# The eight causal lags of a grouped recurrence: sixteen bf16 products over 128 rows, or two sets of four fp32 products over 32 rows each, with a new order of the steps around them

## The reference

```python
ctx = causal_ema(x, tau_ctx)
wg = sigmoid(concat([x, ctx]) @ Wg.T + bg)
gated = x * wg
h1 = gelu(x @ Wn1.T + bn1)                       # 32 hidden values a token
mod = 0.5 + sigmoid(h1 @ Wn2.T + bn2)            # 32 modulations a token
traces = causal_ema(gated * mod[d], tau[d])      # for each of the 32 decays d
temporal = sum_d traces[d] * softmax(blend)[d]
gate = sigmoid(temporal @ Wtemp.T + btemp)
soma = gelu(x @ Wsoma.T + bsoma)
x = x + layernorm((soma * gate) @ Wout.T)
```

## Time and profile before

| | us |
|---|---|
| median of 3 runs (range) | 328.15 (328.13 to 328.81) |
| profiled execution | 326.89 |
| its span | 325.0 |
| front and step 0, TensorE busy | 34.41 of 39.42 |
| steps 1 to 6, TensorE busy | 112.09 of 115.92 |
| end section and attention, TensorE busy | 159.64 of 169.66 |
| steps 1 to 6, VectorE / ScalarE / GpSimd busy | 97.53 / 68.13 / 81.45 |

### The profile page before, as it was taken

How to read it: one execution, slowest core, us unless ns; L and a number is a source line. 1 busy time by engine, 2 the same in 40 slices (tenths; PEclk the granted TensorE clock), 3 DMA queues, 4 the chain that set the end, 5 groups by cost and what they waited for, 6 DMA issues and landing times. The chain is left out here.

```text
span 325.0 us, 9974 instructions
## 1 busy us (share of the span) xinstructions
PE 306.1 (94%) x3314; PEld 207.0 (64%) x3324; DVE 274.6 (85%) x1449; ACT 215.2 (66%) x459; POOL 248.8 (77%) x300
## 2 busy tenths in 40 slices
PE   8898899999999999999887989999999999999995
PEld 2554464656566465555535667887887887887873
DVE  3888899878978886797879669999999999999972
ACT  5862256545655655457674678878778878778863
POOL 3173586778686885665855869999999999999990
PEclk9999999999999999999999999999999999999999
DMA  6700120050311305013530435564544364210011
GB/s 184 222 2 1 32 67 34 17 130 3 105 42 57 90 0 144 4 33 65 75 60 2 87 95 83 82 139 126 126 105 117 93 126 105 78 32 6 3 34 34
DMA packets 29154, 23.07 MB, mean 71 GB/s; under 512 B 2736, under 2 KB 27824, under 8 KB 29104
## 3 DMA queue, kind: packets, MB, share of 16 engines
q1 hardware_dynamic: 29104, 22.44, 29.3%
HBM read 7.75 MB, written 2.10 MB: 30 GB/s over the span
## 5 line engine op out<-in xcount | busy, mean ns | idle before, releaser
L1609 POOL TENSOR_TENSOR arena<-arena,neg_max 128x512 f32<-128x512 f32 x128 | 129.9, 1052 | 10.8 <-DVE neg_max L1451 10.7
L1451 DVE CUSTOM_DVE_ANT_0 arena<-ps,arena 128x128 f32<-128x128 f32 x512 | 113.9, 287 | 9.6 <-issue 5.1
L1093 ACT ACTIVATE arena<-ps 128x512 f32<-128x512 f32 x128 | 69.6, 596 | 10.2 <-PE ps L789 10.2
L789 PE MATMUL ps<-ident_sb,arena 128*128 128x128 f32 x512 | 68.2, 276 | 0.0
L789 PEld LDWEIGHTS ps<-ident_sb,arena 128*128 128x128 f32 x512 | 56.5, 141 | 6.9 <-POOL arena L1609 4.0
L1528 POOL TENSOR_TENSOR arena<-arena 128x448 f32<-128x448 f32 (+6 forms) x56 | 42.8, 764 | 23.2 <-DVE arena L1283 19.6
L1451 DVE DVE_READ_ACCUMULATOR2_ANT neg_max<- 128x1 f32 x512 | 42.6, 83 | 0.0
L805 PE MATMUL ps<-arena 128*32 128x128 f32 x1024 | 41.2, 279 | 0.0
L1515 POOL TENSOR_TENSOR arena<-decay_a,arena 128x192 f32<-128x192 f32 x32 | 19.5, 637 | 22.0 <-ACT arena L930 22.0
L805 PEld LDWEIGHTS ps<-arena 128*32 128x32 f32 x1024 | 24.1, 109 | 6.9 <-issue 0.3
L775 PE MATMUL ps<-arena 48*128 48x128 bf16 x512 | 25.4, 219 | 2.4 <-DVE neg_max L1451 2.3
(11 more groups left out here) (172 smaller groups left out, 575.4 us busy)
## 6 DMA issues: line engine op xcount, KB each, us to landing
arena<-q_parts SPq DMA_DIRECT2D x96, 64.0 KB
arena<-k_parts SPq DMA_DIRECT2D x96, 64.0 KB
arena<-in_x SPq DMA_DIRECT2D x16, 256.0 KB, 3.3
arena<-in_xt SPq DMA_DIRECT2D x8, 256.0 KB, 2.8
out<-arena SPq DMA_DIRECT2D x7, 256.0 KB, 3.0
arena<-in_consts SPq DMA_DIRECT2D x1, 420.0 KB, 3.8
w_sb<-in_w SPq DMA_DIRECT2D x1, 384.0 KB, 6.3
w_sb<-in_w SPq DMA_DIRECT2D x1, 192.0 KB, 4.1
```

Of the source, the lines that this page charges most:

```text
L789: mm = pe.transpose(ps[1][:, q % 2, k * P:k * P + P], neg_t[q % NT_RING][:, k * P:k * P + P], ident)
L1093: act.activation(probT[q % PT_RING], ps[1][:, q % 2, :], ACT.Exp, scale=-1.0)\
L1451: dve.tensor_tensor_reduce(out=neg_t[q % NT_RING][:, cs], in0=ps[0][:, score_bank(c) + slot, cs], in1=nbias[n % 2], scale=1.0, scalar=3.0e ...
L1609: pool.tensor_tensor(t4, t4, neg_max[:, n % 2, 4 * z:4 * z + 4].unsqueeze(2).broadcast_to([P, 4, P]), ALU.subtract).then_inc(s["shifted"], 1)
```

## The change

1. *Lags.* Groups 0 to 7 all use fp32 weights `w_lag` and the fp32 tanh `thd`, on 32 rows a lag. `four_lags` issues four products, lag k of the set on partitions 32k to 32k+31, each into its own bank: lags 0, 1, 6, 7 in banks 0 and 1 of the group's half, lags 2 to 5 in banks 2 and 3 of the other half. All functions that split weights or modulations are gone, and each lag has its own `prod`.
2. *Banks.* The temporal gate uses bank 0 (where the cross products were), the context bank 3, the values bank 3.
3. *Order.* The hidden product (with Wn1) of group g+2 and the query product stand ahead of the output product of group g; the soma product stands behind the local products; on VectorE and ScalarE the steps are re-ordered likewise, and `late_tables` stands ahead of `b_mixed`, the logarithm behind `c_values`.
4. *Step 0* has an order of its own, with a product whose result nobody reads (384 columns) ahead of the output.

```diff
@@ TensorE @@
+            def four_lags(i, m, first):
+                u = m % 2
+                if first == 0:
+                    pe.wait_ge(s["soma_ready"], grp(i, m, 1, 1))
+                    pe.wait_ge(s["modn_ready"], grp(i, m, 1, 1))
+                    if at_start(i, m, 1):
+                        pe.wait_ge(s["vec_step"], vec("lag_c"))
+                        pe.wait_ge(s["h1_ready"], 2)
+                    else:
+                        pe.wait_ge(s["bh_ready"], grp(i, m, NJ + NCAR))
+                else:
+                    pe.wait_ge(s["prod_ready"], grp(i, m, Q, 4))
+                for lag in range(first, first + 4):
+                    rows_of = slice((lag - first) * D, (lag - first) * D + D)
+                    pe.matmul(lag_bank(m, lag), w_lag[rows_of, lag, :], thd[u][rows_of, :], start=True, stop=True)\
+                        .then_inc(s["lag_ps"], 1)
...
-                    pe.wait_ge(s["modT_tanh"], grp(i, m, 1, 1))
...
+                    pe.wait_ge(s["centred"], grp(i, m, GB, -GB))
                 four(ctx_bank(i, m), lambda cs: xn[u][:, cs], lambda cs: lt[:], "ctx_ps")
...
             def b_locals(i, m):
+                if not at_start(i, m, 2):
+                    pe.wait_ge(s["part3_ready"], grp(i, m, 2, -2))
...
             def b_out(i, m):
+                if not last_group(i, m):
+                    pe.wait_ge(s["prod_ready"], grp(i, m, Q, Q + 6))
...
+            def first_step(i, m):
+                b_locals(i, m)
+                f_modulation_n(i, m + 1)
+                f_gate_ctx(i, m + 1)
+                value_bias()
+                b_cross(i, m)
+                four_lags(i, m + 1, 0)
+                b_crossT(i, m)
+                f_gated(i, m + 1)
+                b_gate(i, m)
+                four_lags(i, m + 1, 4)
+                pe.wait_ge(s["gn_ready"], 2)
+                pe.matmul(bank(1, 2)[:, 0:W_FIRST * P], wt["wg_x"], w_sb[:, 0:W_FIRST, :].rearrange("p k c -> p (k c)"),
+                          start=True, stop=True)
+                b_out(i, m)
+                f_hidden(i, m + 2)
+
+            def step(i, m):
...
+                f_modulation(i, m + 1)
+                b_carries(i, m)
+                f_gate_x(i, m + 1)
+                f_context(i, m + 1)
+                b_locals(i, m)
+                f_soma(i, m + 1)
+                f_modulation_n(i, m + 1)
+                f_gate_ctx(i, m + 1)
+                c_x1T(i, m - 1)
+                four_lags(i, m + 1, 0)
+                f_gated(i, m + 1)
+                b_cross(i, m)
+                c_k(i, m - 1)
+                b_crossT(i, m)
+                four_lags(i, m + 1, 4)
+                c_less(i, m - 1, 1, 0)
+                b_gate(i, m)
+                c_less(i, m - 1, 1, 1)
+                c_q(i, m - 1)
+                if not last_group(i, m + 1):
+                    f_hidden(i, m + 2)
+                b_out(i, m)
+                c_less(i, m - 1, 0, 0)
+                c_v(i, m - 1)
+                c_less(i, m - 1, 0, 1)
@@ ScalarE, step @@
-            def f_mod_part1(i, m):
-            def f_mod_part1b(i, m):
...
+                c_part(i, m - 1, 1, 2)
+                c_part(i, m - 1, 0, 0)
+                if not last_group(i, m + 1):
+                    f_hidden(i, m + 2)
+                c_part(i, m - 1, 0, 1)
+                c_values(i, m - 1)
                 if i * 2 + m == COUNTED:
                     act.wait_ge(s["vec_step"], vec("cnt_none"))
                     act.activation(lncnt[:], cnt1[:], ACT.Ln).then_inc(s["lncnt_ready"], 1)
-                if closes:
-                    c_values(i, m - 1)
+                c_part(i, m - 1, 0, 2)
@@ VectorE @@
-            def lag_parts():
-            def f_mod_parts(i, m):
...
+                b_carries(i, m)
+                if at_start(i, m, 2):
+                    key_tables()
                 b_locals(i, m)
                 f_gated(i, m + 1)
+                f_lags(i, m + 1, range(0, 4))
+                b_temporal(i, m)
+                f_lags(i, m + 1, range(4, 6))
                 if first < last:
                     counts(first)
                 if 2 * i + m == COUNTED:
                     late_tables()
+                b_mixed(i, m)
+                f_lags(i, m + 1, range(6, Q))
                 if first < last:
                     counts(first + 1)
                 c_moments(i, m)
+                c_centre(i, m)
@@ GpSimd, step @@
+                f_lags(i, m + 1, range(1, 6))
                 if first < last:
                     counted(first)
+                f_lags(i, m + 1, range(6, Q))
+                c_rstd(i, m)
                 if first < last:
                     counted(first + 1)
```

More of the change, by code:

```diff
@@ L174, in build @@
             gn.append(take(W))
-            prod.append([take(W), take(W)])
+            wide, temporal, two = take(W), take(W), take(W + P // 2)
+            third, fifth, sixth = 5 * W // 8, 3 * W // 8, 2 * W // 8
+            prod.append([None, wide, temporal, two[:, 0:third], two[:, third:], wide[:, 0:fifth],
+                         wide[:, fifth:fifth + sixth], temporal])
             modn.append(take(P))
-            weights_at = at[0] - 4 * W - P
         xn = [take(W) for _ in range(2)]
@@ L188, in build @@
         take(NU * W)
[L189 to L191 removed]
+        crn, temporalT, sg, ln = gn, [p[2] for p in prod], gT, acc
         vx = [take(2 * VS) for _ in range(2)]
@@ L252, in ctx_bank, with lag_bank, gate_bank @@
         def ctx_bank(i, m):
-            return bank(1 if at_start(i, m, 1) else m % 2, 1)
+            return bank(1, 1) if at_start(i, m, 2) else bank(m % 2, 3)
+        def lag_bank(m, lag):
+            return bank(m % 2, lag % 2) if lag in (0, 1, 6, 7) else bank(1 - m % 2, 2 + lag % 2)
+        def gate_bank(i, m):
+            return bank(m % 2, 2 if last_group(i, m) else 0)
         def at_start(i, m, before):
@@ L411, in _ @@
             for _ in range(12):
-                pe.matmul(bank(1, 3), mod_pb[0][:, 0:P], mod_pb[0][:], start=True, stop=True)
+                pe.matmul(bank(1, 3), zeros[:, 0:P], zeros[:, 0:W], start=True, stop=True)
             pe.wait_ge(s["small_loaded"], 32)
@@ L593, in b_gate @@
                 pe.wait_ge(s["temporal_ready"], grp(i, m, 1, 1))
-                pe.matmul(bank(u, 2), wt["wtemp"], temporalT[u], start=True, stop=True).then_inc(s["temp_ps"], 1)
+                pe.matmul(gate_bank(i, m), wt["wtemp"], temporalT[u], start=True, stop=True).then_inc(s["temp_ps"], 1)
             def b_out(i, m):
@@ L730, in repeat @@
                 for _ in range(times):
-                    pe.matmul(bank(0, 2), lag_a[:, 0, :], mod_pa[1][:], start=True, stop=True)
+                    pe.matmul(bank(0, 2), q_parts[:, 0, 0:P], q_parts[:, 0, 0:W], start=True, stop=True)
             def end():
@@ L944, in b_gate @@
                 act.wait_ge(s["temp_ps"], grp(i, m, 1, 1))
-                act.activation(bank(u, 2), bank(u, 2), ACT.Tanh, bias=hb[:, 1:2], scale=0.5).then_inc(s["temp_tanh"], 1)
+                act.activation(gate_bank(i, m), gate_bank(i, m), ACT.Tanh, bias=hb[:, 1:2], scale=0.5).then_inc(s["temp_tanh"], 1)
             def c_x1T(i, m):
@@ L1317, in b_mixed @@
                 dve.wait_ge(s["temp_tanh"], grp(i, m, 1, 1))
-                dve.scalar_tensor_tensor(sg[u], bank(u, 2), 1.0, somaT[u], ALU.add, ALU.mult)\
+                dve.scalar_tensor_tensor(sg[u], gate_bank(i, m), 1.0, somaT[u], ALU.add, ALU.mult)\
                     .then_inc(s["mixed_ready"], 1)
@@ L1378, in step @@
                 first, last = FIRST_QUAD[2 * i + m], FIRST_QUAD[2 * i + m + 1]
-                if closes:
-                    b_carries(i, m)
-                    f_mod_parts(i, m + 1)
+                if not closes:
+                    b_locals(i, m)
+                    f_gated(i, m + 1)
+                    row_factors()
+                    f_lags(i, m + 1, range(0, 2))
+                    b_temporal(i, m)
+                    f_lags(i, m + 1, range(2, 4))
+                    dve.wait_ge(s["const_ps"], 2)
+                    dve.wait_ge(s["rows_loaded"], 16)
+                    pro("kept_bias", dve.tensor_tensor(kept_bias[:], bank(1, 3)[:, 0:P], bo, ALU.add), waited=False)
+                    b_mixed(i, m)
+                    f_lags(i, m + 1, range(4, Q))
+                    c_moments(i, m)
+                    c_centre(i, m)
+                    return
+                b_carries(i, m)
+                if at_start(i, m, 2):
+                    key_tables()
                 b_locals(i, m)
-                if not closes:
-                    row_factors()
                 f_gated(i, m + 1)
-                f_lags(i, m + 1, range(0, 2))
+                f_lags(i, m + 1, range(0, 4))
+                b_temporal(i, m)
+                f_lags(i, m + 1, range(4, 6))
                 if first < last:
```

239 lines of the change are left out of this document (58 added, 181 removed).

## The result

The changed kernel takes 324.13 us (median of 4 executions, 323.15 to 324.38) and the kernel before 328.48 (4 executions, 328.13 to 329.01): 4.35 us less, ratio 0.986, 95% interval 0.983 to 0.989. I had forecast 9.7 us less.

The account below looks back on a forecast made before the run. The prediction took TensorE to bound the groups' stretch. Steps 7.4 us, front 3.4 and the way from last output to end section 0.4, less 1.5 at the end, gave 9.7: 328.15 becomes 318.5 us, range 313.5 to 324.5.

Parts of the forecast that it names:

- sign: Whole kernel: faster by more than 0.2% at 91%, slower by more at 7%, no change at 2%.
- overlap: Lag products on TensorE: a set of four on separate rows was to overlap and take 1.0 us.
- Front and end: Before the first output and in the end section: 3.4 us gained at the front, 1.5 lost at the end.
- Step 6: Last step of the groups: late tables just ahead of the mixing were to lose 0.6 us.
- New order: Reordered steps, followed from the modulation products: a step of 17.9 us, with 17.1 of TensorE work and 0.8 of waiting.
- The order's waits eat TensorE's gain: Local products and output: late waits paid in full, 1.0 us more per step, 324.5 us; chance 17%.
- The late input: Hidden product's input for the group after next: one us late in five steps, 323.5 us; chance 5%.
- TensorE alone decides: Steps and end: only 17.1 us of TensorE work per step stays, the end loses nothing, 312.2 us; chance 11%.

Follow-up runs that it names:

- e5_adj: On e2_swap: turned modulation moved right behind the local products, soma next to the gate product, query product beside the temporal gate's; 318.47 us, ratio 0.971.
- e1_pad: Changed kernel with 22 instead of 11 repeated products in the end section, keeping TensorE busy until the turned x1 of group 6; 321.05 us, ratio 0.980.
- e10_idle: On e2_swap: the 11 repeated products ahead of the turned residual of group 6 removed, so TensorE idles there; 322.33 us.
- e9_fill: On e8_mixfirst: 5, 3 and 4 repeated bf16 products put in three idle stretches of the octets' second and third step; 317.76 us.
- e2_swap: Changed kernel with GpSimd taking the residual of group 6 ahead of the first bias sum; 319.91 us, ratio 0.977.
- e8_mixfirst: On e5_adj: VectorE's late tables of step 6 moved behind the mixing; 319.31 us median, fastest 317.82.
- e3_soma: Changed kernel with the soma product back ahead of the local products in steps 1 to 6; 323.30 us, ratio 0.986.
- e11_rows: Changed kernel with all four lag products of a set on the same 32 rows of TensorE; 367.63 us in one execution.

## Why the prediction was half right

*Bound, sign, overlap.* TensorE bounded the steps before and does after; the set costs 1.07 to 1.08, I had 1.0. By the Trainium skill, "TensorE: Matmul & The Clock Gate", a set was an estimated 1.12; the trace's 1.08 lies between that and my number. The Trainium skill, "TensorEngine Tiling (Array Packing)", section Key Properties, has a change of the tiling mode drain TensorE; the trace agrees in so far as a product next to one of another shape takes longer, as follows, and no run shows that it is a drain.

*Front and end.* First local products at 23.05 (22.75 forecast), first output at 34.33 (34.1): gain 3.17 for 3.4. The turned x1 at 6.14 behind the first scores (6.3), behind ScalarE's bias terms and GpSimd's sum as walked; lost 1.33 for 1.5. Step 6 loses 0.69 to the tables for 0.6.

*The failed step: "New order", the walk to 17.9.* It measured 18.52 to 18.61, six steps 111.5 and not 107.7. That is 3.8 of the missing us. In step 3 against the walk: local products at 4.02 (4.1), the hole 0.51 (0.6), so the dependencies were right. Then local products to gate product 2.48 (2.1); first set at 7.99 (7.9); set and turned gated 1.77 (1.5); from the cross products to the temporal gate's 3.79 (3.6); output at 16.14 (15.6); from there to the next modulation 2.47 (2.3). I had priced every product at its shortest distance in before, 0.86 for one of 512 columns. In the new order more of them stand next to products of 32 rows or 32 columns, or between two bf16 products, and then such a product takes 0.95 or 0.96, and 1.06 for soma, which has one of 32 rows on either side. A turn, or a bf16 product on one side only, adds nothing by itself: 0.86 for e5_adj's gate product ahead of the turned x1, and for before's temporal gate's ahead of a bf16 product (92.19 to 93.05). e5_adj tests the price by regrouping: 0.40 less from the locals to the turned x1, which takes 0.27 of the 0.62 off the step. The rest is spread over places that no run regrouped, and is read from the rows, not tested. The 1.77 also holds the wait of 0.12 for the gated rows, which the walk had not: the gate product was 0.3 late (6.50 for 6.2), and that passed through ScalarE and VectorE.

Two slips in the prediction's own arithmetic decide nothing: 14.85 and 0.86 are 15.7 and not 15.6, and half of the way from 318.5 to 312.2 is 315.4 and not 313.5.

*The missing term: the clock.* I had the hole that GpSimd's residual leaves ahead of the turned x1 as 1.5 us of time and as nothing else, and so put the clock at nothing. The clock fell behind it in the profiled execution, 1.44, and a second time in the attention, about 1.6. e1_pad and e10_idle show that the first needs the hole; for the second that is open. The runs without falls put the gain at 5.6, and 9.7 less the 3.8 of the steps is 5.9. The medians differ by less: the changed kernel's lies 3.1 over its 321.0 without falls, before's own four executions of that comparison 1.9 over its 326.6, and 5.6 + 1.9 - 3.1 is 4.4.

*The rivals.* "The order's waits eat TensorE's gain" gave the time within 0.4 us (324.5), but by a mechanism that was not there: centring and the values' copy were on time. The late input didn't happen. "TensorE alone decides" was wrong in its 17.1 us of work: with the distances as measured it is 17.9 (18.52 less the waits of 0.51 and 0.12).

The best kernel tried, e9_fill (e2_swap, e5_adj, e8_mixfirst and the fills), takes 317.76, ratio to before 0.971 (0.968 to 0.974).

## What to carry to other kernels

Price a TensorE product by the distance of starts with the neighbours that it will have, not by the shortest one in the trace, and put products of one shape and type next to each other. When a moved wait leaves TensorE idle for about 2 us, look at the granted clock behind it, in more than one execution: the products that follow may cost as much again. And before filling a hole, see which chain releases it: in e3_soma the hole only moved from the local products to the lag set. A row that gets shorter gives nothing where the next start waits for another engine, as the temporal gate's in e5_adj; compare each start with the end of what releases it, since a wait of 0.1 is not marked.

## What the runs showed of the hardware

**The clock also fell with TensorE fully busy.** In e11_rows the windows of step 4 read:

```profile
124.00:128.00 4.00, 4.00 (x13) 0.91 0.71 113
128.00:132.00 4.00, 4.00 (x14) 0.50 0.23 30
```

The fall began inside a lag set, 3.7 us of products on a quarter of the rows, with TensorE busy in 4.00 of 4.00 us; the three steps before it had the same sets and no fall. Why in this one stays open.

**A fall in some executions only.** By the mean clock (0.995), e8_mixfirst had the second fall in four of six executions, at idle stretches of 1.16, 0.66 and 1.03 us that are there in each; e1_pad and e2_swap had it in one of six, and e9_fill, with the stretches filled, in none of five. What decides in a single execution, and what makes before's slower ones, stays open.
